# A sparse-expert layer whose sorted rows carry their own destination: results scattered to token order unit by unit, 128-row units, first-layer weights fetched by DMA

## What is computed

```
msg = layernorm(x) @ W + B
s   = exp(-2 * (1/adj - 1)**2) where adj < 1, else 0
x   = x + s @ msg                                  # stage one: reads all of adj

y      = layernorm(x)
top 2 of 16 experts per row by y @ gate_w + gate_b; softmax of the two as shares
h_e(y) = relu(y @ w1[e] + b1[e])                   # 128 -> 256
o_e(y) = h_e(y) @ w2[e] + b2[e]                    # 256 -> 128
x      = x + layernorm(y + sum of share * o_e(y)) * gamma + beta
```

## Time and profile before

| | us |
|---|---|
| median of 3 runs | 1703.95 (1702.5 to 1704.24) |
| the profiled execution, span from its first to its last instruction | 1823.2 |
| mean granted TensorE clock of it, as a share of 2.4 GHz | 0.951 |
| PE busy in it | 1624.7 |
| ACT busy | 1565.7 |
| DVE busy | 1499.7 |
| POOL busy | 463.6 |

### The profile page before, as it was taken

One profiled execution on the slowest core, in us unless ns is written; L12 is line 12 of the kernel. 1 busy time (PEld: TensorE's weight loads), 2 busy tenths in 40 slices (PEclk: granted clock), 3 DMA queues, 4 the chain that ended last, 5 costly groups with the idle time before them and its releaser, 6 DMA issues.

```text
span 1823.2 us, 24195 instructions
## 1 busy us (share of the span) xinstructions
PE 1624.7 (89%) x8178; PEld 1073.6 (59%) x8178; DVE 1499.7 (82%) x2298; ACT 1565.7 (86%) x1502; POOL 463.6 (25%) x342
## 2 busy tenths in 40 slices
PE   4999999999999999999999999999999987384720
PEld 3666666666666666666666656666666786373620
DVE  7999998989899999999999989999998443153464
ACT  5899999999999999999999999999999664253531
POOL 0001223131314040407132231313140213535342
PEclk9999999999999999999999999999999999696765
DMA  9559867676767676776776676787673244343431
GB/s 313 158 160 290 235 199 215 195 217 193 214 195 212 196 212 198 220 213 202 210 202 209 199 210 199 209 247 208 202 206 121 80 124 143 87 141 97 129 110 50
DMA packets 216792, 338.22 MB, mean 186 GB/s; under 512 B 18080, under 2 KB 74144, under 8 KB 216544
## 3 DMA queue, kind: packets, MB, share of 16 engines
q1 hardware_dynamic: 208368, 319.62, 59.8%
q0 software_dynamic: 8304, 17.06, 3.1%
HBM read 303.07 MB, written 33.55 MB: 185 GB/s over the span
## 4 chain that ended last, share of the span: by engine, by line
PE 84%; DVE 6%; another core or an unknown queue 5%; issue 3%; ACT 1%; DMA 1%; DVEq 0%; SPq 0%; ACTq 0%
PE acc L1118 48%; PE tp L1137 24%; PE tp L1164 4%; PE tp L1192 3%; PE acc L1192 2%; DVE chunk L654 1%; PE tp L1153 1%; DVE stats L666 1%; DVE chunk L660 1%; DVE chunk L1004 1%; PE misc L1094 1%; ACT chunk L613 1%; DVE msg L729 1%; DMA xs<-in_x_dram 1%
## 5 line engine op out<-in xcount | busy, mean ns | idle before, releaser
L1118 PE MATMUL acc<-wT,msg 128*128 128x512 f32 x2048 | 976.0, 599 | 0.0
L527 ACT ACTIVATE wT<-tp 128x1024 f32<-128x1024 f32 x512 | 761.0, 1674 | 14.0 <-PE tp L1137 12.4
L521 ACT ACTIVATE chunk<-chunk 128x2048 f32<-128x2048 f32 x256 | 655.3, 2560 | 0.1
L660 DVE SCALAR_TENSOR_TENSOR chunk<-chunk 128x2048 f32<-128x2048 f32 x256 | 584.8, 2284 | 54.7 <-ACT chunk L521 54.1
L1137 PEld LDWEIGHTS tp<-ident,chunk 128*128 128x128 f32 x4096 | 478.7, 141 | 223.2 <-issue 221.5
L654 DVE SCALAR_TENSOR_TENSOR chunk<-chunk 128x2048 f32<-128x2048 f32 x256 | 583.5, 2280 | 1.9 <-DMA chunk<-in_adj_dram 1.9
L1137 PE MATMUL tp<-ident,chunk 128*128 128x128 f32 x4096 | 534.3, 274 | 0.0
L516 ACT ACTIVATE chunk<-chunk 128x4096 f32<-128x4096 f32 x118 | 511.0, 4331 | 0.0
L1118 PEld LDWEIGHTS acc<-wT,msg 128*128 128x128 f32 x2048 | 349.1, 190 | 258.3 <-issue 245.8
L457 POOL TENSOR_TENSOR pool_carrier<-pool_carrier 1x1 f32<-1x1 f32 x32 | 43.7, 1365 | 951.5 <-DVE row_now L845 825.9
L476 POOL DMA_INDIRECT rows_in<-y,row_now x128 | 216.7, 1693 | 40.4 <-issue 40.4
(11 more groups left out here) (121 smaller groups left out, 794.7 us busy)
## 6 DMA issues: line engine op xcount, KB each, us to landing
chunk<-in_adj_dram SPq DMA_DIRECT2D x256, 1024.0 KB, 5.4
chunk<-rows_in SPq DMA_DIRECT2D x118, 64.0 KB
rows_out<-chunk SPq DMA_DIRECT2D x59, 128.0 KB
chunk<-rows_in SPq DMA_DIRECT2D x35, 128.0 KB
rows_out<-chunk SPq DMA_DIRECT2D x17, 256.0 KB
y_kept<-y SPq DMA_DIRECT2D x16, 256.0 KB, 6.1
chunk<-y_kept SPq DMA_DIRECT2D x16, 256.0 KB
out_dram<-chunk SPq DMA_DIRECT2D x16, 256.0 KB
```

Of the source, the lines that this page charges most:

```text
L521: act.activation(slot(c), slot(c), ACT.Exp, scale=-1.0).then_inc(inverted, 1)
L527: act.activation(wT[:, (g * PPG + m) % WSLOTS, :], tp[(g * PPG + m) % TSLOTS][:, :], ACT.Exp, scale=-2.0).then_inc(weighted, 1)
L660: dve.scalar_tensor_tensor(out=slot(c), in0=slot(c), scalar=2.0, in1=slot(c), op0=ALU.subtract, op1=ALU.mult).then_inc(squared, 1)
L1118: ins = pe.matmul(acc[:, :], msg[:, n, :], wT[:, (g * PPG + m) % WSLOTS, k * ROWS:(k + 1) * ROWS], start=(n == 0), stop=(n == 2 * PPG - 1))
```

## The change

Every sorted row gets a 129th number, the row of a new DRAM tensor `by_token` at which its result belongs. `by_token` has the two results of each token next to each other; behind them are spare rows into which the results of padding go. POOL writes those numbers with two `iota` instructions a group into `y_wide`, where y is held twice; a DMA makes the second copy. Padding rows get numbers too, with a DMA of four bytes a row, and each batch's spare units are filled at the start by POOL with DMAs.

When a unit's results are there, POOL scatters them straight to `by_token` (`send`), with the numbers that were loaded with the unit's rows as indices. A group's results then come back with one direct DMA (`load_back`). `store_rows`, the gathers, `row_all`, `row_back` and four of a table's steps are gone. All units have 128 rows; the batches are 8, 5 and 3 groups, 79 + 55 + 39 = 173 units; combines start at steps 91 to 133, 146 to 170 and 185 to 197, all at a pace of 6, of 210 steps. SP loads each unit's w1 from DRAM into its slot (`load_slot`) instead of DVE's copy; ACT reads the bias from `blobs`.

```diff
-    BATCHES = (7, 5, 4)
-    TILES = (1, 2, 1)
-    UR = [t * P for t in TILES]
-    UW = max(UR)
+    BATCHES = (8, 5, 3)
+    UR, UW = P, P
+    WIDE = D + 1
+    SPARE = E - 1
+    DUMPS = len(BATCHES) * (E + SPARE)
...
-    rows_in = nc.dram_tensor("rows_in", [BASE[-1], D], F32).ap()
-    rows_out = [nc.dram_tensor(f"rows_out{b}", [n * UR[b], D], F32).ap() for b, n in enumerate(UNITS)]
+    rows_in = nc.dram_tensor("rows_in", [BASE[-1], WIDE], F32).ap()
+    by_token = nc.dram_tensor("by_token", [K * N + DUMPS * P, D], F32).ap()
+    by_token_v = by_token[0:K * N, :].rearrange("(g b p k) d -> p g b (k d)", b=TB, p=P, k=K)
...
-        SLOTS, RIN, RT, HT, RO, BACK, ZS, FIN = 10, 13, 4, 4, 4, 4, 3, 2
+        SLOTS, RIN, RT, HT, RO, BACK, ZS, FIN = 11, 32, 4, 4, 8, 4, 3, 2
...
-        AT_ONCE, AHEAD = 16, 7
-        GATE_DMAS, EXPERT_DMAS = 4, 4 + FT
+        AT_ONCE, AHEAD, SLOT_AHEAD = 16, 13, 9
+        GATE_DMAS, EXPERT_DMAS = 4, 3 + FT
...
-        COMBINE_WAIT, COMBINE_PACE, COMBINE_LONG = 8, 6, 11
+        COMBINE_WAIT, COMBINE_PACE, COMBINE_LONG = 12, 6, 11
         starts = []
         for b, n in enumerate(BATCHES):
             for _ in range(n):
                 at = UNIT0[b + 1] + COMBINE_WAIT
-                pace = COMBINE_PACE if starts and UR[batch_of(starts[-1])] > P else COMBINE_LONG
-                starts.append(max(at, starts[-1] + pace) if starts else at)
+                starts.append(max(at, starts[-1] + COMBINE_PACE) if starts else at)
...
+                sp.dma_start(y_wide[:, 1, :, 0:D], y[:, :, :]).then_inc(twin_in, 16)
+                sp.dma_start(y_kept[g, :, :].rearrange("p (b d) -> p b d", b=TB), y[:, :, :]).then_inc(y_stored, 16)
...
+                to = rows_in[bass.ds(region_ends[e], UR), :]
+                sp.dma_start(to[:, 0:D], pads[:, :]).then_inc(padded, 16)
...
+                    sp.dma_start(to[:, D:WIDE], pad_ids[:, b * E + e:b * E + e + 1].bitcast(F32)).then_inc(padded, 16)
...
+                    sp.wait_ge(sent[(u - RIN) % RO], ((u - RIN) // RO + 1) * 16)
+                sp.dma_start(rin[u % RIN], rows_in[bass.ds(unit_rows[u], UR), :]).then_inc(rin_full[u % RIN], 16)
+            first_layers = {}
+            def load_slot(u):
                 b = batch_of(u)
...
+                if u == UNIT0[b]:
+                    sp.wait_ge(table_ready, 2 * b + 2)
+                if u == UNIT0[b] or u % AT_ONCE == 0:
...
+                if u >= SLOTS:
+                    sp.wait_ge(hid_full, u - SLOTS + 1)
+                sp.dma_start(slots[u % SLOTS], w1[bass.ds(first_layers[u], 1), :, :].rearrange("a h f -> (a h) f")).then_inc(slot_full[u % SLOTS], 16)
+            def load_back(g):
+                b = max(b for b in range(len(BATCHES)) if FIRST[b] <= g)
+                if g == FIRST[b]:
+                    all_sent(sp, UNIT0[b + 1])
+                if g >= BACK:
+                    sp.wait_ge(back_free, g - BACK + 1)
+                sp.dma_start(back[g % BACK].rearrange("p b k d -> p b (k d)"), by_token_v[:, g, :, :]).then_inc(back_in[g % BACK], 16)
...
-            for u in range(RIN):
+            for u in range(AHEAD):
                 load_rows(u)
+            for u in range(SLOT_AHEAD):
+                load_slot(u)
             sp.wait_ge(turned, STEPS)
             for i in range(LAST + 2):
-                if 1 <= i <= NU:
-                    store_rows(i - 1)
-                if i + RIN < NU:
-                    load_rows(i + RIN)
+                if i + AHEAD < NU:
+                    load_rows(i + AHEAD)
+                if i + SLOT_AHEAD < NU:
+                    load_slot(i + SLOT_AHEAD)
                 if i == 11 * GATE_PACE:
                     store_y(GROUPS - 1)
                 if 0 <= i - PADS_AT < E:
                     pad(len(BATCHES) - 1, i - PADS_AT)
                 for g in range(GROUPS):
-                    if i == starts[g] - COMBINE_PACE:
+                    if i == starts[g] - 1:
                         load_z(g)
+                        load_back(g)
...
+                spare = rows_in[BASE[b + 1] - SPARE * UR:BASE[b + 1], :].rearrange("(s p) d -> p s d", p=P)
+                at = len(BATCHES) * E + b * SPARE
+                pool.dma_start(spare[:, :, 0:D], pads[:, :].unsqueeze(1).to_broadcast([P, SPARE, D])).then_inc(spare_zero, 16)
...
+                    pool.dma_start(spare[:, :, D:WIDE], pad_ids[:, at:at + SPARE].bitcast(F32).unsqueeze(2)).then_inc(spare_zero, 16)
...
+            def name_rows(g):
+                pool.wait_ge(scattered, g * KB * 16)
+                for k in range(K):
+                    pool.iota(y_wide[:, k, :, D].bitcast(I32), pattern=[[K * P, TB]], base=g * K * ROWS + k,
+                              channel_multiplier=K).then_inc(ids_ready, 1)
+            def scatter(g):
                 if g:
                     pool.wait_ge(carried, g)
                 pool.wait_ge(rows_ready, g + 1)
+                pool.wait_ge(twin_in, (g + 1) * 16)
+                pool.wait_ge(ids_ready, (g + 1) * K)
                 carry()
                 for k in range(K):
                     for b in range(TB):
                         pool.indirect_dma_start(
                             rows_in, bass.IndirectOffsetOnAxis(row_now[:, k, b:b + 1].bitcast(U32), 0),
-                            y[:, b, :], None).then_inc(scattered, 16)
...
+                            y_wide[:, k, b, :], None).then_inc(scattered, 16)
+            def send(u):
+                pool.wait_ge(ro_ready, u + 1)
+                pool.indirect_dma_start(
+                    by_token, bass.IndirectOffsetOnAxis(rin[u % RIN][:, D:WIDE].bitcast(U32), 0),
+                    ro[u % RO], None).then_inc(sent[u % RO], 16)
+            for g in range(GROUPS - 1):
+                guess(g)
+                name_rows(g)
+                scatter(g)
+            for u in range(NU):
+                if u == GUESS_AT:
+                    guess(GROUPS - 1)
+                    name_rows(GROUPS - 1)
+                if u == SCATTER_AT:
+                    scatter(GROUPS - 1)
+                send(u)
...
+                    ins = act.activation(hT[u % HT][:, t * UR:(t + 1) * UR], h_bank[u % H_BANKS][:, t * UR:(t + 1) * UR], ACT.Relu,
+                                         bias=blobs[:, bass.ds(hidden_biases[u], 1), B1 + t:B1 + t + 1].rearrange("p a f -> p (a f)"))
...
-                if u >= SLOTS:
-                    dve.wait_ge(hT_ready, u - SLOTS + 1)
-                dve.tensor_copy(slots[u % SLOTS], blobs[:, bass.ds(experts[u], 1), 0:SLOT].rearrange("p a f -> p (a f)")).then_inc(slot_full, 1)
```

More of the change, by code:

```diff
@@ L56, in gnn_moe_kernel @@
     MOST = max(UNITS)
-    PAIRS_OF = [(n + 1) // 2 for n in UNITS]
-    PAIR0 = [sum(PAIRS_OF[:b]) for b in range(len(BATCHES) + 1)]
     KB = K * TB
-    W1, B1, W2, B2 = 0, F, F + FT, F + FT + FT * D
-    SLOT, BLOB = F + FT, B2 + D
+    B1, W2, B2 = 0, FT, FT + FT * D
+    BLOB = B2 + D
     adj_v = adj.rearrange("(g b p) j -> p g b j", b=TB, p=P)
@@ L94, in gnn_moe_kernel @@
         eps = sb("eps", [P, 1])
[L95 removed]
+        pads = sb("pads", [P, D])
+        pad_ids = sb("pad_ids", [P, DUMPS], I32)
         pool_carrier = sb("pool_carrier", [1, 3])
@@ L229, in gnn_moe_kernel @@
         rT_ready = sem("rT_ready")
-        slot_full = sem("slot_full")
+        slot_full = [sem(f"slot_full{i}") for i in range(SLOTS)]
         hid_full = sem("hid_full")
@@ L234, in gnn_moe_kernel @@
         ro_ready = sem("ro_ready")
-        ro_out = [sem(f"ro_out{i}") for i in range(RO)]
+        sent = [sem(f"sent{i}") for i in range(RO)]
         back_in = [sem(f"back_in{i}") for i in range(BACK)]
@@ L466, in guess @@
                 pool.tensor_tensor(rs[:, 0, :], spread[:, :], minus_half[:, :], ALU.pow).then_inc(guessed, 1)
-            for g in range(GROUPS):
-                guess(g)
+            def name_rows(g):
[4 more added lines that the diff above has]
+            def scatter(g):
                 if g:
@@ L1030, in _ @@
             dve.wait_ge(turned, (GROUPS - 1) * PPG + PPG - RING // 2 * PAIRS)
-            for u in range(AHEAD):
-                fetch(u)
+            fetch(0)
             gate_sum(GROUPS - 1)
```

196 lines of the change are left out of this document (73 added, 123 removed).

## The result

The changed kernel takes 1768.82 us (1764.96 to 1771.45) against 1703.22 us (1702.08 to 1704.24) before: a ratio of 1.0386, 95% interval 1.0371 to 1.0401. It is slower by 65.6 us, where 1715 with a range to 1748 had been forecast: the direction was right, the size far off. The profiled execution has a span of 1766.9 us and a time of its own of 1768.63 us, so here the trace can be laid against the times as it stands. No stretch like those of the earlier trace rows is in it.

A forecast was written before the change was run, and what follows sets the result against it. It took PE to bound stage one, and queues of nearly equal speed the units. Second stage 2 + 122 + 127 + 33 + 1 = 285 us against 274.3, so 1719.0 by the trace, 1715 timed; range 1682 to 1748.

The forecast's parts named there:

- The stretches: Second stage before: nine stretches, 114.9 us, all but POOL nearly still; taken as recording effect. Rival, real: 1755, chance 0.06.
- I take 1, since it is a burst beside 8 MB of prefetch.: Start of stage one: writing about 3 MB of spare rows during the first chunk loads costs 1 us.
- its own worst case of 10: Start: upper bound of 10 us for the spare rows' writes, their bytes at 294 GB/s.
- Steps 0 to 90 ... I take 122.: Second stage, 91 units without a combine: 122 us, between 114 and 130, plus 2 for the first unit.
- the queues' sums: Steps 0 to 90: POOL's work adds to 126 us, 116 with PE eight sends ahead; SP's to 124.
- Steps 91 to 172 at 1.55: Second stage, 82 units beside combines: 1.55 us each, set by the DMA engines; 127 us, 114 to 137.
- The end.: After the last unit: last send, landing, load, three combines and last store, 33 us (28 to 38), before 58.
- Stage one hides POOL's additions.: Stage one: POOL's added scatters, iotas, second y copy and two batches' pads lie beside PE's stream.
- Rows off their boundaries: Rival: 516-byte row loads cost 0.13 to 0.25 us more a unit in steps 91 to 172; 1726 to 1735, chance 0.12.
- the prediction's estimate of up to half as much again: Row loads of 516 bytes cost up to 0.38 us a unit instead of 0.25; sum about 10 us more, 1725.
- The clock: Rival: TensorE granted 1.2 GHz, so a unit takes 2.0 us, 0.45 above 1.55; 1752, chance 0.03.
- POOL alone as the pace: Faster rival: only POOL's 1.25 us a unit sets the second stage, other queues fill gaps; 1694, chance 0.21.

The follow-up runs named there:

- b1: Kernel before the change, with combines at a pace of 8 instead of 11 steps where units have 128 rows: 1710.78 us.
- e1: Changed kernel with all six writes of spare rows issued behind group 2's scatter instead of at the start: 1758.19 us.
- e2: Changed kernel with only the spare rows' four-byte destination numbers written behind group 2's scatter, the zeros still at the start: 1760.35 us.
- e6: Changed kernel with the spare rows' writes issued one batch at a time, behind the scatters of groups 3, 6 and 9: 1743.94 us.
- e3: Changed kernel with results loaded six steps ahead of their combine instead of one, and first combines 18 steps behind the batch's last unit instead of 12: 1763.57 us.
- f2: e6 with the last batch's 16 paddings on every third step from 66 to 111 instead of every step from 66 to 81: 1748.08 us.
- f3: e6 with the loads of first-layer weights, all but the first nine, issued by ScalarE instead of SyncE: 1730.64 us.
- d1: e6 with each unit loading only half of its first-layer weights (64 KB instead of 128) and using them twice: 1744.33 us.
- b2: Kernel before the change, with 4 instead of 8 gathers a group: 1701.18 us.
- e4: Changed kernel with first-layer weights back in SBUF and copied to their slots by VectorE, seven units ahead: 1739.03 us.
- e5: Changed kernel with the edits of e4 and e6 together: 1713.67 us.
- d2: e5 with batches of 9, 5 and 2 groups instead of 8, 5 and 3: 1726.25 us.
- f4: e5 with 18 buffers for results instead of 8, and the first batch's combines 12 steps later: 1708.63 us.
- d3: e5 with only every second unit's results sent, the combine reading y from its own tensor in place of results: 1696.82 us.

## Why the prediction was wrong

- *The stretches are no part of the timed runs.* Right (b1, and the changed kernel's own time beside its span).
- *"I take 1, since it is a burst beside 8 MB of prefetch."* This step failed first: 21 us, above its own worst case of 10. Shown by e1, e2 and e6. The bound divided the bytes by the full rate of adj's reads, 294 GB/s, but writes and reads together moved only 161 to 186 GB/s there; and what the chunks lose at the start, PE, which is the bound for the next 1390 us, never makes up. With the late step of 5 us below, these are the 25 us of unit 0.
- *"Steps 0 to 90 ... I take 122."* The second step that failed: 141.6. POOL's 1.25 us a send was right (1.26), SyncE's issue nearly (0.54 for 0.50), and so were the queues' sums. Wrong was to take about the larger of two queues' sums for all 91 units, and to put the wait for the first results at nothing. The limits follow each other: units 0 to 66 go at POOL's pace (90.6; 66 x 1.25 and 10 are 93; with half the sends 76.3, with 18 buffers 71.1), units 66 to 91 at SyncE's (16 paddings of 2.20 us where a send has 1.26), and VectorE stands 10 us for a load that SyncE issues behind all that. e3, f2 and f3 change these 51 us (to 42.7, 43.3 and 33.4).
- *Steps 91 to 172 at 1.55, "where the DMA engines are".* Right in size by luck (127.7 for 127), wrong in the reason: d1 takes bytes away and gains nothing, f3 takes issues from SyncE and gains 5, copied weights 9 to 13. With SyncE relieved and half the sends gone, 116.9 stay, and what sets those is open.
- *The end.* 36.2 for 33, as reckoned: sends, landing, a load, three combines. Before, 58 was near too (57.8 in b1, 61.6 in b2).
- *Stage one hides POOL's additions.* Nearly. In the changed kernel and in e1, e3, e4, e5 and f2 VectorE's next y waits for POOL and its scatters once while the last group is read, and PE takes some 5 us longer for eight matmuls into `acc` (10.59 in the changed kernel). This is the late step; d2 has such steps at two other places. In the changed kernel:

```profile
1401.81 1.11 DVE L819 TENSOR_SCALAR y_wide<-xs,mv_now,rs 128x128 f32<-128x128 f32 x4 [2.48 <-DMA rows_in<-y_wide,row_now]
```

  The eight scatters ahead of it take 35 us, and 18 before. They take 35 in every profile of the changed scheme with batches of 8, 5 and 3, also in those in which PE is not late, so they alone don't decide it. In the changed kernel three of the eight take 8.67, 6.52 and 7.57 us; what holds them up is open.
- *Rivals.* Rows off their boundaries: a little, and not what decided. SyncE's queue (packets, MB, share of 16 engines), before from 1440 to 1490 us, with rows of 512 bytes, and in e5 from 1440 to 1530, mostly with rows of 516:

```profile
q1 hardware_dynamic: 13262, 6.41, 46.5%
```

```profile
q1 hardware_dynamic: 12950, 5.42, 25.9%
```

  In full that is 276 and 233 GB/s. Packet by packet the traces have a mean of 35 ns for 516 bytes and 29 for 512, with medians of 28 and 27: most rows cost next to nothing more, some a lot, and all together about a fifth. That is within the prediction's estimate of up to half as much again, and below its rival. And as d1 shows, bytes did not set the time. The clock: between its two levels, with a mean of 0.95, 0.87 and 0.90 of 2.4 GHz in the three windows of units, where PE was busy for 0.83, 0.70 and 0.76 of the time, and 1.00 in f4's units 0 to 66, where it was busy for 0.98. The rival had 0.50 throughout; what the lower clock cost is not separated by any run. POOL alone as the pace, the rival that ended faster at 1694: not reached. With SyncE's weight loads gone, e5 and f4 stand at 1713.67 and 1708.63, and only without half of the sends, in d3, it is 1696.82.

## What to carry to other kernels

Work that is moved "to the start, where nothing runs" lies in front of the first loads; ask what the bound engine of the next stage waits for, and spread such writes in pieces that the prefetch can cover. Where several queues bound a stage in turn, add up the stretches with the limit of each, and look at the instruction that comes behind the longest run of issues on an in-order queue: a load placed one step ahead of its use is late by all that stands before it. To tell a queue's issues from its bytes, halve the bytes, and then move the issue to another engine.

## What the runs showed of the hardware that was not expected

- Writes of zeros and of four-byte numbers from POOL's queue (2.9 MB, rows 516 bytes apart) beside reads of adj: full DMA engines at 161 and 186 GB/s, where they move 342 and 337 without them (e6). Packets were served one for one: 460 of POOL's, 465 of SyncE's in 15 us.
- Half the bytes of a load with as many pieces: DMA share 0.80 to 0.71, time unchanged.
- SyncE's direct loads and stores of this size: 0.54 us from issue to issue, so that four a unit, 2.20 us, were the limit while the DMA engines had a share of about 0.65 (the third window of the changed kernel).
